# Reciprocal square roots on ACT as exp(-ln/2), and a product of queries and keys that does not wait for its masks, in a fused decoder layer

## The chip, the cores and the metric

The kernel runs on one core of a Trainium2 chip. The metric is the device time of one execution in microseconds, from the first to the last of the program's work. TensorE (PE) multiplies matrices, VectorE (DVE), ScalarE (ACT) and GpSimd (POOL) do elementwise work, and SyncE (SP) issues the transfers. Each engine has its own in-order list of instructions; engines wait for one another through semaphores.

## The reference, cut to what matters

64 sequences of 128 tokens with 512 features pass through one decoder layer: attention with 16 heads, a second mixing stage against a context (an mLSTM), a gated choice of one of eight small experts, and a layer norm after each of the three.

```python
x = _layernorm(x + attn(x, Wq, bq, Wk, bk, Wv, bv, Wo, bo))
x = _layernorm(x + mlstm(x, ctx, ctx, Wi, bi, Wf, bf, ln_scale))
x = _layernorm(x + ffn(x, ...))
# _layernorm: (x - m) / sqrt(v + 1e-5), over the 512 features
# inside mlstm, for every head:
qk = einsum('bhsd,bhtd->bhst', qh, kh) / sqrt(dh)
C = qk * D                      # D is zero above the diagonal
normalizer = maximum(abs(C.sum(-1)), exp(-max_log_D))
h = einsum('bhst,bhtd->bhsd', C / (normalizer + EPS), vh)
hn = (h - mu) * rsqrt(var + EPS)   # mean and variance over a head's 32 features
```

So a tile needs four reciprocal square roots: one per token in each of the three layer norms, and one per token and head (16 columns) in the mLSTM.

## The kernel before, in words

A tile is one sequence: 128 tokens on the partitions, 512 features in a row. Seven tiles are in flight at once. In step a the kernel works on tile a and its six elders, called b (one older) to g (six older): the projections of a, the attention of b up to its layer norm x1, the gates and the decay matrix Dx of c, the mLSTM's result of d, its layer norm x2 and the experts' products of e, their choice for f, and the last layer norm and the store for g. Nothing schedules this at run time: each engine has a hand-written `step(a)` that names the pieces in the order in which that engine does them, and the order of the five lists is what the kernel is tuned by. The first 10 steps are unrolled, the next 54 run in a loop with two steps in its body, and 6 more drain the pipeline. POOL's list is counted one step behind the others, so its `c` is the others' `d`.

In the loop a wait stands only where the code says `wait_ge`; the waits in `edge(...)` are written out in unrolled steps alone, because in the loop another wait or an engine's own order already implies them.

The pieces that the change and the prediction name:

- TensorE, at the end of a step: the projection of the keys `p_k` (L376 is its last group), `m_QK` (L478, the product of the context's queries and keys, into the four banks of `quad`), the transposes of x1 `m_x1T` (L365), the experts' first product, the next tile's transposes, the gates `m_gate` (L458, L460), and then the attention's scores `a_S` (L412 lays down a mask, L418 multiplies). In the middle of a step `m_H` (L500) makes the mLSTM's result and `x_Y` (L526) the experts' second product; L526 waits until ACT has copied the result of L500 out of its banks (`Hs`, L659).
- DVE: `norm_stats` makes mean and variance (L926, L929, and `ve` in L931), `a_x1` (L946) the normalized x1, `p_KT` (L875) a transpose, `m_C` (L969) the product of `quad` and the masked Dx, in four parts in the order 1, 3, 0, 2; `r_y` (L992) multiplies by `h_rs`.
- ACT: `m_Dx` (L652) makes Dx as 16 exponentials, `x_yo` (L690) the output row from `rs3` and `nm3`, `m_x1T` (L622) a copy.
- POOL: four powers with exponent -0.5 (L777 for 128x16, L791 for 128x1), `m_mask` (L762, the zeros above the diagonal of Dx, four parts), `r_y2` (L781), `r_r2` (L786), `x_nm` (L814, minus mean times `rs3`).

Before the first tile TensorE runs 62 small products on ones to warm up (WARM), between two steps of the set-up.

Of the kernel before, what the change touches and what calls it, by code (L numbers as in the profile page):

```python
# [27 lines left out]
P = 128  # L28
# [3 lines left out]
H = 16  # L32
# [22 lines left out]
PADS = 5  # L55
PEEL = 10
WARM = 62
# [47 lines left out]
def bass_decoder(nc, x, ctx, wq, wk, wv, wo, bqkv, bo, rope, ident, mask_l, mask_r, head_rows,  # L105
                 w_gate, b_gate, ln_scale, w_expert, debias, degen, expert_rows, out):
    with ExitStack() as stack:
# [3 lines left out]
        def sem(name):  # L111
# [23 lines left out]
        half_neg = sb("half_neg", [P, H])  # L135
# [19 lines left out]
        ve1 = sb("ve1", [P, 1])  # L155
        rs1 = sb("rs1", [P, 1])
# [28 lines left out]
        h_ve = sb("h_ve", [P, H])  # L185
        h_rs = sb("h_rs", [P, H])
# [3 lines left out]
        ve2 = sb("ve2", [P, 1])  # L190
        rs2 = sb("rs2", [P, 1])
# [26 lines left out]
        ve3 = sb("ve3", [P, 1])  # L218
        rs3 = sb("rs3", [P, 1])
# [140 lines left out]
        def _(pe):  # L360
# [223 lines left out]
        def _(act):  # L584
# [106 lines left out]

            nc.scalar.preload_act_table_set("natural_log_exp_and_others")
# [10 lines left out]
            def step(a):  # L703
# [37 lines left out]
                if b.real():  # L741
                    m_x1T(b)
# [4 lines left out]
        def _(pool):  # L747
# [53 lines left out]
            def x_score(t):  # L801
                pool.wait_ge(s.fn3_sb, upto(t))
                tt(f_s[:], f_sc[:], f_n3[:], ALU.mult).then_inc(s.fs_sb, 1)
# [3 lines left out]
                edge(pool, t, (s.fe_sb, 1))  # L807
# [9 lines left out]
            nc.gpsimd.memset(half_neg[:], -0.5).then_inc(s.pads_set, 1)  # L817
# [15 lines left out]
            def step(a):  # L833
# [13 lines left out]
                if d.real():  # L847
                    rsqrt(d, ve2, rs2, s.ve2_sb, s.rs2_sb, s.x2_sb)
# [6 lines left out]
                if c.real():  # L855
                    r_pow(c)
                if f.real():
                    rsqrt(f, ve3, rs3, s.ve3_sb, s.rs3_sb, s.yo_sb)
                    x_nm(f)
# [8 lines left out]
        def _(dve):  # L868
# [385 lines left out]
```

## Time and profile before

| what | value |
|---|---|
| runs | 1709.47, 1708.28, 1704.01 us; median 1708.28 |
| profiled execution | 1706.93 us, of which the span of the trace is 1705.2 us |
| busy over the span | PE 1520.7 us (89%), DVE 1283.2 (75%), POOL 955.2 (56%), ACT 855.4 (50%) |
| chain that ended last | POOL 31%, PE 25%, DVE 21%, issue 19% |
| stage up to 91 us | set-up and first tile, PE busy 36.19 us |
| 91 to 335 us | unrolled steps, PE busy 219.66 of 244 us |
| 335 to 1640 us | the loop, PE busy 1233.26 of 1305 us, granted clock 1.00 |
| 1640 to 1705.2 us | the drain, PE busy 31.63 of 65.2 us, granted clock 0.65 |

A busy share says how long an engine worked, not whether it set the pace: the chain follows from the last instruction back to whatever released each wait. The loop holds more than three quarters of the time and its steps are alike, so one step read closely stands for 54.

### The profile page before, as it was taken

The page shows a single profiled execution, that of the slowest core. Times are in us where ns is not written, and L with a number is a line of the kernel's source. Part 1 is how long each engine was busy: PE and PEld are TensorE (multiplying, and loading weights), DVE is VectorE, ACT ScalarE, POOL GpSimd, SP SyncE. Part 2 cuts the span into 40 slices and gives each one's busy share as a digit, 9 for nine tenths or more (in the row PEclk, how much of TensorE's full clock was granted, in tenths as well). Part 3 has the DMA queues.
Part 4 walks back from the last instruction along what each step waited for, and adds up shares of the span by engine and source line. Part 5 has one row for each costly group of instructions (what it writes and reads, how often), then busy time and mean ns, then how long its engine had stood idle before and what let it go on. Part 6 is the DMA issues. An engine that isn't in the chain of part 4 may idle for free.

```text
span 1705.2 us, 67667 instructions
## 1 busy us (share of the span) xinstructions
PE 1520.7 (89%) x27398; PEld 1196.0 (70%) x27398; DVE 1283.2 (75%) x3337; ACT 855.4 (50%) x2385; POOL 955.2 (56%) x1232
## 2 busy tenths in 40 slices
PE   0789999999999999999999999999999999999955
PEld 0667777777777777777777777777777777777743
DVE  4346777787787778777877787778778877877764
ACT  2035545545554555455545554555555455645551
POOL 1025556555655665566556655665565556556653
PEclk9899999999999999999999999999999999999985
DMA  4123333333433343333233333333343334333310
GB/s 155 38 84 106 105 105 101 108 105 99 123 103 106 99 123 98 112 99 122 96 104 109 118 99 95 120 108 105 96 123 105 105 99 123 102 108 99 105 58 31
DMA packets 195142, 174.71 MB, mean 102 GB/s; under 512 B 141887, under 2 KB 143551, under 8 KB 186890
## 3 DMA queue, kind: packets, MB, share of 16 engines
q1 hardware_dynamic: 195082, 173.87, 33.4%
q8 instruction: 42, 0.69, 0.2%
q14 instruction: 18, 0.15, 0.0%
HBM read 139.76 MB, written 34.08 MB: 102 GB/s over the span
## 4 chain that ended last, share of the span: by engine, by line
POOL 31%; PE 25%; DVE 21%; issue 19%; ACT 2%; SPq 1%; POOLq 1%; DMA 0%; DVEq 0%; ACTq 0%
POOL h_rs L777 12%; POOL Dx L762 5%; PE quad L418 5%; POOL rs L791 4%; POOL r L786 4%; DVE Dx L969 3%; PE bank L365 3%; PE bank L513 2%; PE bank L490 2%; PE bank L458 2%; PE bank L526 2%; POOL nm L814 2%; POOL c L770 2%; PE bank L373 2%; PE bank L374 2%
## 5 line engine op out<-in xcount | busy, mean ns | idle before, releaser
L757 POOL TENSOR_TENSOR ex<-ex,w_rec 128x512 f32<-128x512 f32 x64 | 67.2, 1050 | 543.7 <-DVE w_rec L910 543.7
L652 ACT ACTIVATE Dx<-Mb,a_col 128x128 f32<-128x128 f32 x1024 | 312.9, 395 | 7.6 <-DMA Mb<-m_rows 7.4
L777 POOL TENSOR_TENSOR h_rs<-h_ve,half_neg 128x16 f32<-128x16 f32 x64 | 207.1, 3236 | 8.5 <-DVE h_ve L987 1.7
L622 ACT ACTIVATE x1T<-bank 128x512 f32<-128x512 f32 x64 | 38.2, 597 | 314.4 <-PE bank L365 314.4
L762 POOL TENSOR_SCALAR_AFFINE_SELECT Dx<-Dx 128x512 f32<-128x512 f32 x256 | 159.9, 636 | 8.6 <-ACT Dx L652 8.6
L969 DVE SCALAR_TENSOR_TENSOR Dx<-quad,Dx 128x512 f32<-128x512 f32 x256 | 157.1, 668 | 7.3 <-PE quad L478 7.3
L946 DVE TENSOR_SCALAR x<-r,mv,rs 128x512 f32<-128x512 f32 x64 | 54.3, 849 | 129.6 <-POOL rs L791 129.6
L791 POOL TENSOR_TENSOR rs<-ve,half_neg 128x1 f32<-128x1 f32 x192 | 104.8, 546 | 37.7 <-DVE ve L931 37.6
L659 ACT ACTIVATE Hs<-quad 128x528 f32<-128x528 f32 x64 | 39.1, 611 | 171.3 <-PE quad L500 171.3
L478 PE MATMUL quad<-x1T,cT 32*128 32x128 f32 x2048 | 76.6, 286 | 43.3 <-issue 26.9
L373 PE MATMUL bank<-wq_high,x_high 128*128 128x512 f32 x256 | 115.1, 449 | 0.0
L373 PE MATMUL bank<-wv_high,x_high 128*128 128x512 f32 x256 | 114.3, 446 | 0.0
L478 PEld LDWEIGHTS quad<-x1T,cT 32*128 32x128 f32 x2048 | 66.0, 189 | 68.7 <-POOL Dx L762 66.3
L373 PE MATMUL bank<-wk_high,x_high 128*128 128x512 f32 x256 | 112.8, 441 | 0.0
L431 PEld LDWEIGHTS quad<-PT,VG 32*32 32x32 f32 x8192 | 74.9, 103 | 53.0 <-issue 52.3
L373 PE MATMUL bank<-wo_high,O_high 128*128 128x512 f32 x256 | 106.8, 417 | 0.0
L374 PE MATMUL bank<-wo_low,O_high 128*128 128x512 f32 x256 | 102.7, 401 | 0.0
L374 PE MATMUL bank<-wq_low,x_high 128*128 128x512 f32 x256 | 102.2, 399 | 0.0
L365 PE MATMUL bank<-id_sb,x 128*128 128x128 f32 x512 | 82.5, 284 | 21.4 <-DVE x L946 11.3
L374 PE MATMUL bank<-wk_low,x_high 128*128 128x512 f32 x256 | 101.1, 395 | 0.0
L374 PE MATMUL bank<-wv_low,x_high 128*128 128x512 f32 x256 | 100.8, 394 | 0.0
L936 DVE TENSOR_TENSOR r<-bank,xr 128x512 f32<-128x512 f32 x64 | 44.3, 692 | 73.5 <-PE bank L376 73.5
(163 smaller groups left out, 4357.4 us busy)
## 6 DMA issues: line engine op xcount, KB each, us to landing
Mb<-m_rows SPq DMA_DIRECT2D x64, 1024.0 KB, 4.6
xb<-in_x SPq DMA_DIRECT2D x256, 64.0 KB
xr<-in_x SPq DMA_DIRECT2D x64, 256.0 KB, 3.0
cb<-in_ctx SPq DMA_DIRECT2D x64, 256.0 KB, 2.6
v_rows<-v_sb SPq DMA_DIRECT2D x64, 256.0 KB, 3.3
VG<-v_rows SPq DMA_DIRECT2D x64, 256.0 KB, 3.9
out_dram<-yo SPq DMA_DIRECT2D x64, 256.0 KB, 3.1
Dx<-in_wq SPq DMA_DIRECT2D x4, 256.0 KB, 4.7
```

Source lines behind the costliest of these rows:

```text
L365: last = nc.tensor.transpose(dst[:, c * P:(c + 1) * P], src[:, c * P:(c + 1) * P], id_sb[:])
L373: mm(bank[b][:], high[:, c, :], w_high[n][:, c, :], start=first and c == 0, stop=False)
L374: mm(bank[b][:], high[:, c, :], w_low[n][:, c, :], start=False, stop=False)
L418: last = mm(quad[32 * c:32 * c + 32, w, 32 * v:32 * v + 32], QT[rows, cols], KT[rows, cols], start=False, stop=True, skip_group_check=True ...
L431: last = mm(quad[32 * w:32 * w + 32, c, 32 * v:32 * v + 32], VG[rows, w, v, :], PT[rows, w, v, :], start=True, stop=True, skip_group_check ...
L478: last = mm(quad[:, j, n * P:(n + 1) * P], cT[t.parity()][rows, n, :], x1T[t.parity()][rows, n, :], start=True, stop=True)
L652: last = go(Dx[t.parity()][:, j, n, :], Mb[t.parity()][:, h, :], ACT.Exp, bias=a_col[t.parity()][:, h:h + 1], scale=-1.0)
L762: nc.gpsimd.affine_select(Dx[t.parity()][:, j], Dx[t.parity()][:, j], compare_op=ALU.is_ge, fill=0.0, base=0, pattern=[[0, CH], [1, P]], c ...
L777: tt(h_rs[:], h_ve[:], half_neg[:], ALU.pow).then_inc(s.hrs_sb, 1)
L786: tt(r2[:], r2[:], x1[t.parity()][:], ALU.add).then_inc(s.r2_sb, 1)
L791: tt(rs[:], ve[:], half_neg[:, 0:1], ALU.pow).then_inc(rs_sem, 1)
L969: stt(out=Dx[t.parity()][:, j], in0=quad[:, j, :].rearrange("p (c n) -> p c n", n=P), scalar=float(D) ** -0.5, in1=Dx[t.parity()][:, j], o ...
```

## The change

The four powers leave POOL. In their place ACT computes ln(ve) into a new small tile and then exp(-0.5 ln), as two activations joined by a semaphore. `n_2` stands on ACT ahead of `m_Hs`, `n_h` behind the first quarter of Dx, `n_3` behind the copy of x2's transposes, `n_1` at the end of the step ahead of the copy of x1's transposes. `m_QK` no longer waits for the masks. On POOL the fourth mask now directly follows the third, mask 2 of the next tile stands ahead of `r_y2`, and `x_nm` stands behind it. Two waits that the old order implied are written out: x1 waits for the addition r2 of two tiles before, and POOL's score for the previous exponential. There are 68 warming products in place of 62, and one memset fewer.

```diff
-PADS = 5
+PADS = 4
-WARM = 62
+WARM = 68
             def m_QK(t):
-                for j in range(3):
-                    pe.wait_ge(s.Dm_sb[j], upto(t))
                 edge(pe, t, (s.x1T_sb, 0), (s.cT_sb, 0), (s.sub_sb, -1), (s.Ohigh_sb, -1), (s.Olow_sb, -1))
...
+            def rsqrt(t, ve, ln, rs, ve_sem, ln_sem, rs_sem, used):
+                act.wait_ge(ve_sem, upto(t))
+                go(ln[:], ve[:], ACT.Ln).then_inc(ln_sem, 1)
+                act.wait_ge(ln_sem, upto(t))
+                edge(act, t, (used, 1))
+                go(rs[:], ln[:], ACT.Exp, scale=-0.5).then_inc(rs_sem, 1)
+            def n_1(t):
+                rsqrt(t, ve1, ln1, rs1, s.ve1_sb, s.ln1_sb, s.rs1_sb, s.x1_sb)
...
-            def r_pow(t):
-                pool.wait_ge(s.hve_sb, upto(t))
-                edge(pool, t, (s.y1_sb, 1))
-                tt(h_rs[:], h_ve[:], half_neg[:], ALU.pow).then_inc(s.hrs_sb, 1)
-            def rsqrt(t, ve, rs, ve_sem, rs_sem, used):
-                pool.wait_ge(ve_sem, upto(t))
-                edge(pool, t, (used, 1))
-                tt(rs[:], ve[:], half_neg[:, 0:1], ALU.pow).then_inc(rs_sem, 1)
             def x_score(t):
                 pool.wait_ge(s.fn3_sb, upto(t))
+                pool.wait_ge(s.fe_sb, upto(t, 1))
...
-            nc.gpsimd.memset(half_neg[:], -0.5).then_inc(s.pads_set, 1)
             def a_x1(t):
                 dve.wait_ge(s.rs1_sb, upto(t))
-                edge(dve, t, (s.r2_sb, 2), (s.x1T_ps, 2))
+                dve.wait_ge(s.r2_sb, upto(t, 2))
+                edge(dve, t, (s.x1T_ps, 2))
```

On ACT, in the loop, around the copy Hs of the mLSTM's result (HT, ex and cT are other copies and the attention's exponential; ve is the variance of x2's norm). Before:

```order
L617 ACTIVATE HT<-bank 128x512 [waits HT_ps]
L601 ACTIVATE ex<-ex 128x512 [waits sub_sb]
L659 ACTIVATE Hs<-quad 128x528 [waits H_ps]
L612 ACTIVATE cT<-bank 128x512 [waits cT_ps]
L664 ACTIVATE h_abs<-Hs 128x16 [waits Hs_sb]
```

and after, the same stretch:

```order
L618 ACTIVATE HT<-bank 128x512 [waits HT_ps]
L602 ACTIVATE ex<-ex 128x512 [waits sub_sb]
L695 ACTIVATE ln<-ve 128x1 [waits ve2_sb]
L698 ACTIVATE rs<-ln 128x1 [waits ln2_sb]
L660 ACTIVATE Hs<-quad 128x528 [waits H_ps]
L613 ACTIVATE cT<-bank 128x512 [waits cT_ps]
L665 ACTIVATE h_abs<-Hs 128x16 [waits Hs_sb]
```

Two activations, the first with a wait for ve2, stand ahead of Hs. On ACT at the end of a step, from the copy of x2's transposes on. Before:

```order
L674 ACTIVATE x2T<-bank 128x512 [waits x2T_ps]
L595 REGISTER_ALU [waits v_ps]
L596 ACTIVATE v_sb<-bank 128x512 [waits v_out]
L652 ACTIVATE Dx<-Mb,a_col 128x128 x4
L689 REGISTER_ALU [waits nm3_sb]
L690 ACTIVATE yo<-y_0,nm,rs 128x512 [waits y_out]
L622 ACTIVATE x1T<-bank 128x512 [waits x1T_ps]
```

and after:

```order
L675 ACTIVATE x2T<-bank 128x512 [waits x2T_ps]
L695 ACTIVATE ln<-ve 128x1 [waits ve3_sb]
L698 ACTIVATE rs<-ln 128x1 [waits ln3_sb]
L596 REGISTER_ALU [waits v_ps]
L597 ACTIVATE v_sb<-bank 128x512 [waits v_out]
L653 ACTIVATE Dx<-Mb,a_col 128x128 x4
L690 REGISTER_ALU [waits nm3_sb]
L691 ACTIVATE yo<-y_0,nm,rs 128x512 [waits y_out]
L695 ACTIVATE ln<-ve 128x1 [waits ve1_sb]
L698 ACTIVATE rs<-ln 128x1 [waits ln1_sb]
L623 ACTIVATE x1T<-bank 128x512 [waits x1T_ps]
```

The pair for the last norm stands ahead of the copy of v, the pair for x1 behind yo. On POOL, in the loop, from the context's product c to the masks (h_rs and rs are the powers, r the mLSTM's result on its way to x2). Before:

```order
L770 TENSOR_TENSOR c_1<-cb,a_col 128x16x31 [waits HT_ps,c_in1,acol_sb]
L777 TENSOR_TENSOR h_rs<-h_ve,half_neg 128x16 [waits hve_sb]
L789 REGISTER_ALU
L791 TENSOR_TENSOR rs<-ve,half_neg 128x1 [waits ve3_sb]
L814 TENSOR_SCALAR nm<-mv,rs 128x1 [waits rs3_sb,pads_set]
L781 TENSOR_TENSOR r<-r,lns_sb 128x512 [waits y1_sb]
L762 AFFINE_SELECT Dx<-Dx 128x512 [waits Dx_sb2,pads_set]
L786 TENSOR_TENSOR r<-r,x_0 128x512 [waits x1_sb,y2_sb]
L762 AFFINE_SELECT Dx<-Dx 128x512 [waits Dx_sb0,pads_set]
L762 AFFINE_SELECT Dx<-Dx 128x512 [waits Dx_sb1,pads_set]
L791 TENSOR_TENSOR rs<-ve,half_neg 128x1 [waits ve1_sb]
```

and after:

```order
L798 TENSOR_TENSOR c_1<-cb,a_col 128x16x31 [waits HT_ps,c_in1,acol_sb]
L790 AFFINE_SELECT Dx<-Dx 128x512 [waits Dx_sb2,pads_set]
L804 TENSOR_TENSOR r<-r,lns_sb 128x512 [waits y1_sb]
L832 TENSOR_SCALAR nm<-mv,rs 128x1 [waits rs3_sb,pads_set]
L809 TENSOR_TENSOR r<-r,x_0 128x512 [waits x1_sb,y2_sb]
L790 AFFINE_SELECT Dx<-Dx 128x512 [waits Dx_sb0,pads_set]
L790 AFFINE_SELECT Dx<-Dx 128x512 [waits Dx_sb1,pads_set]
L790 AFFINE_SELECT Dx<-Dx 128x512 [waits Dx_sb3,pads_set]
```

The powers are gone, mask 2 has moved ahead of the multiplication by lns_sb and nm behind it. TensorE's list differs only in the waits of L478 and in the count of warming products.

## Rows read from the trace of the kernel before

**Rows 1.** One step: stretch, length, busy PE, PEld, DVE, ACT, POOL, clock, DMA, GB/s

```profile
1004.69:1029.20 24.51, 23.14 (x427) 18.38 (x428) 19.54 (x51) 13.19 (x37) 14.84 (x20) 1.00 0.36 110
```

**Rows 2.** Waits in 52 loop steps: total us, times, longest us

```profile
PE quad L478 <- issue: 24.5, 41, 0.6
...
PE quad L412 <- DVE Dx L969: 9.3, 26, 0.4
PE bank L365 <- DVE x L946: 8.7, 51, 0.2
...
PE quad L478 <- POOL Dx L762: 6.9, 11, 0.6
```

**Rows 3.** Timeline of TensorE, end of a step: start, us, line, operation, idle before

```profile
1002.98 1.08 PE L376 MATMUL bank<-wk_high,x_low 128*128 128x512 f32 x4
1004.69 1.17 PE L478 MATMUL quad<-x1T,cT 32*128 32x128 f32 x32 [0.63 <-POOL Dx L762]
...
1008.90 0.27 PE L460 MATMUL bank<-cT,wg_ctx 128*48 128x128 f32 x1
1009.53 0.24 PE L412 MATMUL quad<-pair_r,pair_l 32*128 32x128 bf16 x4 [0.36 <-DVE Dx L969]
```

**Rows 4.** Timeline of POOL in the same step

```profile
995.72 3.24 POOL L777 TENSOR_TENSOR h_rs<-h_ve,half_neg 128x16 f32<-128x16 f32 x1
...
999.66 0.64 POOL L814 TENSOR_SCALAR nm<-mv,rs 128x1 f32<-128x1 f32 x1 [0.18 <-POOL rs L791]
1000.26 1.29 POOL L781 TENSOR_TENSOR r<-r,lns_sb 128x512 f32<-128x512 f32 x1
...
1002.12 1.29 POOL L786 TENSOR_TENSOR r<-r,x 128x512 f32<-128x512 f32 x1
1003.36 1.23 POOL L762 TENSOR_SCALAR_AFFINE_SELECT Dx<-Dx 128x512 f32<-128x512 f32 x2
```

**Rows 5.** Timeline of TensorE, first step of the loop

```profile
341.72 1.08 PE L376 MATMUL bank<-wk_high,x_low 128*128 128x512 f32 x4
342.73 1.17 PE L478 MATMUL quad<-x1T,cT 32*128 32x128 f32 x32
```

**Rows 6.** Timeline of DVE in the step of rows 3

```profile
991.27 0.15 DVE L931 TENSOR_SCALAR ve<-mv 128x1 f32<-128x1 f32 x1
...
999.48 0.68 DVE L992 TENSOR_TENSOR r<-Hs,h_rs 128x512 f32<-128x512 f32 x1
...
1002.83 0.15 DVE L931 TENSOR_SCALAR ve<-mv 128x1 f32<-128x1 f32 x1
1005.13 0.84 DVE L946 TENSOR_SCALAR x<-r,mv,rs 128x512 f32<-128x512 f32 x1 [2.15 <-POOL rs L791]
1005.90 1.07 DVE L875 STREAM_TRANSPOSE KT<-bank 128x512 f32<-128x512 f32 x1
1006.83 2.44 DVE L969 SCALAR_TENSOR_TENSOR Dx<-quad,Dx 128x512 f32<-128x512 f32 x4
```

**Rows 7.** Timeline of ACT in the same step

```profile
986.30 0.31 ACT L633 ACTIVATE g_exp<-g_abs 16x128 f32<-16x128 f32 x1
...
986.85 0.29 ACT L637 ACTIVATE g_ln<-g_exp 16x128 f32<-16x128 f32 x1
...
991.63 0.61 ACT L659 ACTIVATE Hs<-quad 128x528 f32<-128x528 f32 x1 [2.73 <-PE quad L500]
...
994.22 0.18 ACT L643 ACTIVATE eFM<-bank 128x16 f32<-128x16 f32 x1
...
1000.92 0.82 ACT L690 ACTIVATE yo<-y,nm,rs 128x512 f32<-128x512 f32 x1
```

**Rows 8.** Timeline of TensorE, the experts' product of the same step

```profile
992.39 1.10 PE L526 MATMUL bank<-degen_sb,LT 72*128 72x512 f32 x2 [0.17 <-ACT Hs L659]
```

**Rows 9.** Timeline of ACT, start of the kernel

```profile
0.81 1.28 ACT L692 ACT_TABLE_LOAD   x1 [0.81 <-PEq L1245]
```

**Rows 10.** Timeline of TensorE, warming products

```profile
42.34 6.47 PE L532 MATMUL bank<-ones_bf 128*128 128x128 bf16 x62 [42.34 <-DVE wx_prod L1123]
```

More of the change, by code:

```diff
@@ L134, in bass_decoder @@
         xrow_sb = sb("xrow_sb", [P, 3, NX])
-        half_neg = sb("half_neg", [P, H])
         xb = [sb(f"xb{i}", [P, E]) for i in range(2)]
@@ L155, in bass_decoder @@
         ve1 = sb("ve1", [P, 1])
+        ln1 = sb("ln1", [P, 1])
         rs1 = sb("rs1", [P, 1])
@@ L185, in bass_decoder @@
         h_ve = sb("h_ve", [P, H])
+        h_ln = sb("h_ln", [P, H])
         h_rs = sb("h_rs", [P, H])
@@ L190, in bass_decoder @@
         ve2 = sb("ve2", [P, 1])
+        ln2 = sb("ln2", [P, 1])
         rs2 = sb("rs2", [P, 1])
@@ L218, in bass_decoder @@
         ve3 = sb("ve3", [P, 1])
+        ln3 = sb("ln3", [P, 1])
         rs3 = sb("rs3", [P, 1])
@@ L229, in bass_decoder @@
             S_ps max_sb sub_sb ex_sb sum_sb rec_sb exn_sb PT_sb
-            O_ps Ohigh_sb Olow_sb proj_ps r1_sb st1_sb mv1_sb ve1_sb rs1_sb x1_sb
+            O_ps Ohigh_sb Olow_sb proj_ps r1_sb st1_sb mv1_sb ve1_sb ln1_sb rs1_sb x1_sb
             x1T_ps x1T_sb cT_ps cT_sb c1_sb gate_ps gs_sb gsum_sb gabs_sb gexp_sb gln_sb
             Fs_sb a_sb M_sb FM_sb aT_ps acol_sb QK_ps HT_ps HT_sb H_ps Hs_sb sq_sb
-            habs_sb hn1_sb hn2_sb hnn_sb hvar_sb hve_sb hrs_sb y1_sb y2_sb r2_sb
-            st2_sb mv2_sb ve2_sb rs2_sb x2_sb rs2sq_sb
+            habs_sb hn1_sb hn2_sb hnn_sb hvar_sb hve_sb hln_sb hrs_sb y1_sb y2_sb r2_sb
+            st2_sb mv2_sb ve2_sb ln2_sb rs2_sb x2_sb rs2sq_sb
             x2T_ps x2T_sb F_ps fz_sb fz2_sb fn1_sb fn2_sb fn3_sb fs_sb fu_sb fv_sb fe_sb fe1_sb
             gate_sb gmax_sb gkey_sb gkmax_sb oh_sb L_sb LT_ps LT_sb Y_ps y3_sb st3_sb mv3_sb
-            ve3_sb rs3_sb nm3_sb yo_sb""".split()
+            ve3_sb ln3_sb rs3_sb nm3_sb yo_sb""".split()
         four = "Dx_sb Dm_sb C_sb".split()
@@ L690, in x_yo, with n_h, n_2, n_3 @@
                 go(yo[:], y3[t.parity()][:], ACT.Identity, bias=nm3[:], scale=rs3[:]).then_inc(s.yo_sb, 1)
+            def rsqrt(t, ve, ln, rs, ve_sem, ln_sem, rs_sem, used):
[6 more added lines that the diff above has]
+                rsqrt(t, ve1, ln1, rs1, s.ve1_sb, s.ln1_sb, s.rs1_sb, s.x1_sb)
+            def n_h(t):
+                rsqrt(t, h_ve, h_ln, h_rs, s.hve_sb, s.hln_sb, s.hrs_sb, s.y1_sb)
+            def n_2(t):
+                rsqrt(t, ve2, ln2, rs2, s.ve2_sb, s.ln2_sb, s.rs2_sb, s.x2_sb)
+            def n_3(t):
+                rsqrt(t, ve3, ln3, rs3, s.ve3_sb, s.ln3_sb, s.rs3_sb, s.yo_sb)
             nc.scalar.preload_act_table_set("natural_log_exp_and_others")
@@ L715, in step @@
                     a_exp(b)
+                if e.real():
+                    n_2(e)
                 if d.real():
@@ L730, in step @@
                     m_Dx(c, 2)
+                if d.real():
+                    n_h(d)
+                if c.real():
                     m_Dx(c, 0)
@@ L734, in step @@
                     x_x2T(e)
+                if g.real():
+                    n_3(g)
                 if a.real():
@@ L741, in step @@
                 if b.real():
+                    n_1(b)
                     m_x1T(b)
@@ L806, in x_score @@
                 pool.wait_ge(s.fu_sb, upto(t))
-                edge(pool, t, (s.fe_sb, 1))
                 tt(f_v[:], f_u[:], xrow_sb[:, 1, :], ALU.mult).then_inc(s.fv_sb, 1)
@@ L839, in step @@
                     m_mask(c, 1)
-                if b.real():
-                    rsqrt(b, ve1, rs1, s.ve1_sb, s.rs1_sb, s.x1_sb)
-                if c.real():
                     m_mask(c, 3)
@@ L846, in step @@
                     a_scale(a)
-                if d.real():
-                    rsqrt(d, ve2, rs2, s.ve2_sb, s.rs2_sb, s.x2_sb)
                 if e.real():
@@ L854, in step @@
                     m_c1(b)
[L855 to L859, printed above, removed]
+                if b.real():
+                    m_mask(b, 2)
                 if c.real():
                     r_y2(c)
-                if b.real():
-                    m_mask(b, 2)
+                if f.real():
+                    x_nm(f)
             steps(pool, step)
```

## Prediction

> **What bounds the kernel now.** I read the busy time of one step first, then the table of waits over the loop, then the timelines of one step engine by engine. One pass of the loop body for one tile lasts 24.51 us, and TensorE is busy in 23.14 of them at granted clock 1.00, so at its full level of 2.4 GHz [rows 1]. The kernel is therefore nearly TensorE bound, and only TensorE's holes can be won: 24.51 - 23.14 = 1.37 us a step. The waits say whose they are [rows 2]. Over 52 steps TensorE stands idle before the product of queries and keys (L478) for 24.5 + 6.9 = 31.4 us, 0.60 a step; before the transposes of x1 8.7 us, 0.17 a step; before the attention scores (L412), held by DVE's product with Dx, 9.3 us, 0.18 a step. In the timeline of one step the last product ends at 1002.98 + 1.08 = 1004.06, L478 starts at 1004.69 [rows 3]; POOL's masks 0 and 1 end at 1003.36 + 1.23 = 1004.59 [rows 4]. So L478 waits for the masks, though "issue" is named in 41 of 52 steps. Of the masks' lateness POOL's power of 3.24 us is one link, but the multiplication by lns_sb (L781) that follows waits for DVE as well: DVE's r ends at 999.48 + 0.68 = 1000.16, L781 starts at 1000.26 [rows 4, 6].
>
> **The change part by part.** All times are on the axis of that one step.
>
> Product without masks: how L478 starts when the masks are already there is shown at the loop's first step: the product before it ends at 341.72 + 1.08 = 342.80 and L478 starts at 342.73, 0.07 before that end [rows 5]. So the term is 0.60 + 0.07 = 0.67 us a step. Bounds: 0.53, were it to start 0.07 behind instead, and 0.70 from the step shown (1004.69 - 1003.99). What is late next is x1.
>
> x1 and the scores: x1 starts at 1005.13 after 2.15 us of waiting for POOL's rs, which lies behind the masks [rows 6]. Its variance is ready at 1002.83 + 0.15 = 1002.98. The new pair, Ln and Exp of 128x1, stands on ACT after yo. The nearest row is an Exp of 128x16 at 0.18 us; the dearest are Exp and Ln of 16x128 at 0.31 and 0.29 [rows 7]. With three handovers of at most 0.10 (DVE's r to POOL's L781, above) the pair takes 0.45 to 0.90 us; I take 0.5, nearer to the 128x16 row. ACT must be free: yo now waits for nm, which stands behind L781: 1000.26 + 1.29 + 0.64 = 1002.19, and yo takes 0.82, to 1003.05 with a handover. rs would then be there at 1003.5 to 1003.6. x1 has a new wait too, r2 of two tiles before: L781, nm and the addition L786 one after the other, 1000.26 + 1.29 + 0.64 + 1.29 = 1003.48, with a handover 1003.58 [rows 4]. Both paths end at 1003.6, so x1 moves 1.5 us forward. Behind it on DVE are the transpose KT (0.77 later) and Dx (0.93 after that) [rows 6]: Dx could start at 1005.30. L478 would end at 1003.99 + 1.17 = 1005.16, so x1's transposes find their input: 0.17 saved, and 0.07 for the same running together of two products. The masks 0 and 1 end at 1003.48 + 1.23 = 1004.71, before DVE wants them. The scores: before, Dx ends at 1006.83 + 2.44 = 1009.27 and L412 starts at 1009.53, 0.26 later, while the gate's products end at 1008.90 + 0.27 = 1009.17 [rows 3, 6]. After, Dx ends at 1007.74 and would let L412 go at 1008.00; TensorE gets there at 1005.16 + (1009.17 - 1005.86 - 0.17) - 0.07 = 1008.23, less 0.07. So TensorE is last again and the 0.18 go, with 0.07: 0.25. DVE's spare time there is only 0.16 us, which is the thin place of this forecast.
>
> What it costs: n_2's pair stands on ACT ahead of Hs, and Hs holds TensorE: the experts' product L526 waits 0.17 us for it [rows 8]. ve2 is ready at 991.27 + 0.15 = 991.42, Hs starts at 991.63 [rows 6, 7]. With 0.04 to 0.10 to hand over, two activations of 0.18 and a step between them, Hs starts at 991.77 if it overlaps with the Exp and at 991.95 if not: 0.14 to 0.32 later; I take 0.20. With the dear rows it would be 0.5; below nothing it can't be, since no work is taken off ACT. The other two pairs lie beside slack: h_rs is wanted by DVE's r at 999.48, and POOL took its variance up at 995.72, so ACT has 3.8 us for it; rs3 is wanted after L781, at 1000.26 + 1.29 = 1001.55. On POOL the power of 3.24 us and three of one column go, on ACT 8 x 0.18 = 1.4 us of busy time come; POOL's saving is worth nothing by itself, since L781 still waits for DVE's r at the same place.
>
> What a table would cost is weighed here too. The trace has one table load, 1.28 us, at the start of ACT [rows 9], and Exp L633 and Ln L637 lie 0.55 us apart in start with another activation between [rows 7]: no load fits. The Trainium skill, "ScalarE: Activation LUTs", section "Table sets: the hidden batching unit", says that one set is active at a time and that natural_log_exp_and_others has both Exp and Ln. The trace agrees; by that page ("What ACT_TABLE_LOAD costs") a change of set would be 2.66 us, an estimated 21 us for eight a step, had they lain in two sets.
>
> Start: six more warming products. 62 of them take 6.47 us [rows 10], so six take 0.63 us, and the copy that follows is on DVE's way to the weights' low parts, so I count them: +0.6, bounds 0 and 0.63.
>
> The sum: per step -0.67 - 0.24 - 0.25 + 0.20 = -0.96 us. The loop has 54 steps: -51.8. The eight unrolled steps with this product and the drain get, as an estimate from the same terms, -3 (bounds 0, since code is issued less evenly there, and -13, all terms in full). With the start: -54. The profiled execution took 1706.93 us (span 1705.2, the 1.7 around it unchanged): 1653. Its time lies between the lowest run (1704.0) and the median (1708.3); against the median the sum gives 1654. I say 1653.
>
> **Rivals.** First, the wait moves to x1 on DVE. For it: yo, r2 and rs all end within 0.1 us of each other, and only 0.16 us is spare. Against it: each of these was added with its full duration. If x1 comes half a microsecond later (1004.1), L412 starts 0.34 later: -0.62 a step, -33 in the loop, -2 outside, 1672. At 1.0 us later the step saves 0.12 and the time is 1698.
>
> Second, the masks hold the end as before. DVE's Dx needs them whatever TensorE does, and they still follow L781 and L786. They would have to end 0.75 us (1005.30 - 1004.71 + 0.16) later than worked out to undo anything; then the scores wait where the product waited, and at 0.96 more all is as before: 1707. Little speaks for it, since POOL has one power fewer in that stretch.
>
> Third, slower: ACT holds TensorE. ACT works in order, and Hs, the context's copy, O_high and all of Dx now stand behind a wait for ve2. At present ve2 is 0.21 us ahead of Hs. The gains other than this are 0.67 + 0.24 + 0.25 = 1.16 us; the kernel is slower once Hs starts more than 1.16 us later, so once ve2 comes 0.84 (1.16 - 0.32) us later against TensorE. At 1.5 us later Hs slips 1.82 us: -1.16 + 1.82 = +0.66 a step, +36, 1743. Against it: DVE's rows from the scores to ve2 follow one another without the change touching any of them, and r2, which the statistics need, is written at 1003.41 now, 12 us before ve2's next turn.
>
> Fourth, slower by tables: eight loads of 1.28 us [rows 9] are 10.2 us of ACT a step, two of them ahead of Hs: -1.16 + 0.20 + 2.56 = +1.6 a step, 1793. Only the row speaks of the price, nothing for the case.
>
> **How the numbers follow.** The forecast gets 0.70, the wait moved to x1 0.20, the masks 0.04, ACT holding TensorE 0.05, tables 0.01. The forecast alone: -1.16 + 0.14 a step with -13 outside gives 1639; the dear pair (0.5 for Hs) gives -0.66 a step and, with nothing outside, 1671. A cheaper start of L412 in full (0.36 in the step shown) is inside the first. The range reaches into the first rival: 1638 to 1682, with about 1 in 10 above it and somewhat less below. A change of 0.3% is 5 us, about what a measurement of this kernel can tell from none. Faster: 0.70 + 0.18 of the first rival = 0.88; same: 0.02 + 0.03 = 0.05; slower: 0.05 + 0.01 + 0.01 = 0.07.
>
> **What would show it.** In the changed kernel's timeline L478 should start within 0.1 us of the product's end, with 0.6 us gone; the step should be 23.5 to 23.6 us. x1 should start about 1.5 us earlier against the product's end, and its wait should name ACT's rs or POOL's r2. L412 should follow the gate's products without a wait for Dx. Hs should start 0.1 to 0.3 us later against ve2, and L526's wait grow from 0.17 to about 0.37. POOL should be busy for less than 14.84 - 3.24 = 11.6 us a step, ACT for about 13.19 + 1.4 = 14.6. The forecast is wrong if TensorE still shows a wait of 0.3 us or more before L412 or x1's transposes (first rival), if L412 waits for masks (second), or if L526's wait is over 1 us (third).

## The result and the profile after

The changed kernel takes 1634.1 us (median of 1634.38, 1636.49, 1633.84 and 1633.58), the kernel before 1708.9 beside it: a ratio of 0.956 [0.952, 0.960]. The forecast was 1653 with a range from 1638 to 1682. The direction and the place were right, the size was not: the gain is 75 us, where 54 were forecast.

The page of the changed kernel, busy times of the engines and the chain of waits:

```profile
PE 1503.2 (92%) x27277; PEld 1192.3 (73%) x27404; DVE 1284.0 (79%) x3337; ACT 947.2 (58%) x2897; POOL 629.5 (39%) x975
...
PE 72%; DVE 18%; issue 5%; ACT 4%; SPq 1%; DMA 0%; POOL 0%; DVEq 0%; POOLq 0%
```

POOL, 31% of the chain before, is off it; TensorE has gone from 25% to 72%. One step of the loop, in the columns of [rows 1], with which it compares:

```profile
984.18:1007.50 23.32, 22.95 (x428) 18.32 (x429) 19.63 (x52) 14.62 (x45) 9.84 (x16) 1.00 0.37 112
```

A step is 1.2 us shorter (24.51 before). POOL lost 5.0 us of busy time and ACT took 1.4. Of the waits of TensorE over the loop [rows 2] one kind is left that counts:

```profile
PE bank L527 <- ACT Hs L660: 14.5, 51, 0.3
```

The end of a step on TensorE (L479 was L478, L368 was L365, L415 was L412, L463 was L460), to set beside [rows 3]:

```profile
983.15 1.10 PE L379 MATMUL bank<-wk_high,x_low 128*128 128x512 f32 x4
984.18 1.17 PE L479 MATMUL quad<-x1T,cT 32*128 32x128 f32 x32
985.28 0.66 PE L368 MATMUL bank<-id_sb,x 128*128 128x128 f32 x4
...
988.15 0.27 PE L463 MATMUL bank<-cT,wg_ctx 128*48 128x128 f32 x1
988.36 0.23 PE L415 MATMUL quad<-pair_r,pair_l 32*128 32x128 bf16 x4
```

L479 starts 0.07 us before the key product's end (983.15 + 1.10 = 984.25), the transposes 0.07 before L479's, the scores 0.06 before the gate's (988.42). All three holes are closed. DVE and POOL in the same stretch, beside [rows 6] and [rows 4]:

```profile
982.99 0.15 DVE L940 TENSOR_SCALAR ve<-mv 128x1 f32<-128x1 f32 x1
983.65 0.98 DVE L956 TENSOR_SCALAR x<-r,mv,rs 128x512 f32<-128x512 f32 x1 [0.51 <-ACT rs L698]
984.55 1.06 DVE L884 STREAM_TRANSPOSE KT<-bank 128x512 f32<-128x512 f32 x1
985.48 1.85 DVE L979 SCALAR_TENSOR_TENSOR Dx<-quad,Dx 128x512 f32<-128x512 f32 x3
```

```profile
980.38 1.30 POOL L804 TENSOR_TENSOR r<-r,lns_sb 128x512 f32<-128x512 f32 x1 [2.81 <-DVE r L1002]
981.65 0.27 POOL L832 TENSOR_SCALAR nm<-mv,rs 128x1 f32<-128x1 f32 x1
981.88 1.30 POOL L809 TENSOR_TENSOR r<-r,x 128x512 f32<-128x512 f32 x1
983.12 2.00 POOL L790 TENSOR_SCALAR_AFFINE_SELECT Dx<-Dx 128x512 f32<-128x512 f32 x3
```

x1 waits 0.51 us for its scale, where it waited 2.15 [rows 6]. The second of the three masks of the last row ends at about 984.45 (two thirds of 2.00), 0.2 us behind the key product: it is still late for L479, which only no longer waits for it. ACT, the pair ahead of Hs and the pair for x1:

```profile
971.51 0.20 ACT L695 ACTIVATE ln<-ve 128x1 f32<-128x1 f32 x1 [2.55 <-DVE ve L940]
971.74 0.20 ACT L698 ACTIVATE rs<-ln 128x1 f32<-128x1 f32 x1
971.85 0.59 ACT L660 ACTIVATE Hs<-quad 128x528 f32<-128x528 f32 x1
...
983.18 0.20 ACT L695 ACTIVATE ln<-ve 128x1 f32<-128x1 f32 x1 [0.32 <-DVE ve L940]
983.41 0.20 ACT L698 ACTIVATE rs<-ln 128x1 f32<-128x1 f32 x1
```

Each activation of 128x1 takes 0.20 us, the second starts 0.23 behind the first, and an activation that doesn't depend on the second (Hs) starts 0.11 behind it.

Where the 72.5 us between the two spans came from is read at one instruction of every step, DVE's addition that begins x1's norm. Before, at tiles 0, 9, 10, 62 and 63:

```profile
86.97 0.69 DVE L936 TENSOR_TENSOR r<-bank,xr 128x512 f32<-128x512 f32 x1 [5.82 <-PE bank L376]
...
312.66 0.69 DVE L936 TENSOR_TENSOR r<-bank,xr 128x512 f32<-128x512 f32 x1 [0.99 <-PE bank L376]
...
339.83 0.69 DVE L936 TENSOR_TENSOR r<-bank,xr 128x512 f32<-128x512 f32 x1 [1.67 <-PE bank L376]
...
1614.16 0.69 DVE L936 TENSOR_TENSOR r<-bank,xr 128x512 f32<-128x512 f32 x1 [0.95 <-PE bank L376]
...
1639.61 0.69 DVE L936 TENSOR_TENSOR r<-bank,xr 128x512 f32<-128x512 f32 x1 [2.09 <-PE bank L376]
```

and after:

```profile
86.71 0.69 DVE L945 TENSOR_TENSOR r<-bank,xr 128x512 f32<-128x512 f32 x1 [4.44 <-PE bank L379]
...
302.48 0.69 DVE L945 TENSOR_TENSOR r<-bank,xr 128x512 f32<-128x512 f32 x1 [1.05 <-PE bank L379]
...
328.41 0.69 DVE L945 TENSOR_TENSOR r<-bank,xr 128x512 f32<-128x512 f32 x1 [1.48 <-PE bank L379]
...
1540.85 0.69 DVE L945 TENSOR_TENSOR r<-bank,xr 128x512 f32<-128x512 f32 x1 [0.97 <-PE bank L379]
...
1567.32 0.69 DVE L945 TENSOR_TENSOR r<-bank,xr 128x512 f32<-128x512 f32 x1 [1.60 <-PE bank L379]
```

The start gives 0.3 us; the nine unrolled steps 225.69 - 215.77 = 9.9; the 53 steps from tile 9 to tile 62, which lie in the loop, 1301.50 - 1238.37 = 63.1, 1.19 each; the step from tile 62 to tile 63 loses 1.0 and the drain gains 0.2. (The loop is longer than the stretch from 335 to 1640 us that I had called by its name: TensorE's branch at the end of a pass stands at 345.2 for the first time and at 1620.3 for the last, so the loop begins at about 295. The step of [rows 5] is the second of the loop's first pass.)

### The profile page after: what moved, and what is told of

It is laid out like the page before. It is cut to its first block, busy times and chain, and to the rows that moved or that the text cites. A ratio compares the mean times of both kernels' runs of the same rounds, so it can differ in the third digit from the quotient of the medians.

```text
span 1632.7 us, 67814 instructions
## 1 busy us (share of the span) xinstructions
PE 1503.2 (92%) x27277; PEld 1192.3 (73%) x27404; DVE 1284.0 (79%) x3337; ACT 947.2 (58%) x2897; POOL 629.5 (39%) x975
## 4 chain that ended last, share of the span: by engine, by line
PE 72%; DVE 18%; issue 5%; ACT 4%; SPq 1%; DMA 0%; POOL 0%; DVEq 0%; POOLq 0%
PE bank L376 13%; PE bank L377 12%; PE bank L379 11%; PE bank L368 6%; PE quad L421 5%; PE quad L434 5%; PE bank L527 5%; PE quad L479 4%; PE bank L461 4%; PE bank L514 4%; DVE w_sum L914 2%; DVE neg_max L905 2%; DVE ex L910 2%; DVE st L935 2%; ACT Hs L660 2%
## 5 line engine op out<-in xcount | busy, mean ns | idle before, releaser
L653 ACT ACTIVATE Dx<-Mb,a_col 128x128 f32<-128x128 f32 x1024 | 317.6, 388 | 4.1 <-DMA Mb<-m_rows 4.1
L790 POOL TENSOR_SCALAR_AFFINE_SELECT Dx<-Dx 128x512 f32<-128x512 f32 x256 | 167.2, 677 | 89.4 <-ACT Dx L653 89.4
L695 ACT ACTIVATE ln<-ve 128x1 f32<-128x1 f32 x192 | 38.1, 199 | 198.2 <-DVE ve L940 198.2
L804 POOL TENSOR_TENSOR r<-r,lns_sb 128x512 f32<-128x512 f32 x64 | 82.6, 1291 | 173.5 <-DVE r L1002 109.2
L527 PE MATMUL bank<-degen_sb,LT 72*128 72x512 f32 x128 | 76.0, 677 | 20.5 <-ACT Hs L660 15.2
L368 PE MATMUL bank<-id_sb,x 128*128 128x128 f32 x512 | 82.4, 284 | 9.2 <-DVE x2sq L1018 7.0
L421 PE MATMUL quad<-KT,QT 32*32 32x32 f32 x8192 | 83.4, 200 | 5.8 <-issue 5.8
L434 PE MATMUL quad<-PT,VG 32*32 32x32 f32 x8192 | 82.8, 201 | 6.2 <-issue 5.9
L935 DVE BATCH_NORM_STATS2 st<-r 128x6 f32<-128x512 f32 x128 | 85.3, 666 | 3.9 <-POOL r L809 1.6
```

What stands on the lines that cost most here:

```text
L368: last = nc.tensor.transpose(dst[:, c * P:(c + 1) * P], src[:, c * P:(c + 1) * P], id_sb[:])
L421: last = mm(quad[32 * c:32 * c + 32, w, 32 * v:32 * v + 32], QT[rows, cols], KT[rows, cols], start=False, stop=True, skip_group_check=True ...
L434: last = mm(quad[32 * w:32 * w + 32, c, 32 * v:32 * v + 32], VG[rows, w, v, :], PT[rows, w, v, :], start=True, stop=True, skip_group_check ...
L527: mm(bank[6][:], LT[:], degen_sb[:], start=True, stop=True).then_inc(s.Y_ps, 1)
L653: last = go(Dx[t.parity()][:, j, n, :], Mb[t.parity()][:, h, :], ACT.Exp, bias=a_col[t.parity()][:, h:h + 1], scale=-1.0)
L790: nc.gpsimd.affine_select(Dx[t.parity()][:, j], Dx[t.parity()][:, j], compare_op=ALU.is_ge, fill=0.0, base=0, pattern=[[0, CH], [1, P]], c ...
```

## The experiments

My theory was: x1's chain (its power, x1, the transpose KT, Dx, the scores) and the wait for the masks held TensorE in two places that lie one behind the other, so that taking out the first wait gains nothing without the second edit; what is left is the pair ahead of Hs; and POOL's lighter load is worth nothing by itself. The rivals: the parts add up; POOL's lighter load carries part of the gain.

**The mask wait alone.** The kernel before, without the waits; the two waits that the old order implied (for r2 at x1, and for the previous exponential at POOL's score) are written out as in the changed kernel:

```diff
 def m_QK(t):
-    for j in range(3):
-        pe.wait_ge(s.Dm_sb[j], upto(t))
...
```

> The kernel before, with all four powers left on POOL, and only the waits of the product of queries and keys for the masks taken out. Theory (the two edits work only together): the product starts 0.67 us earlier in each step, but the transposes of x1 behind it still wait for x1, whose power stands behind the masks on POOL; the engine's idle time moves from the one place to the other, and the end of the step stays: 1708 us, within 4 us. Rival (the parts add up): 54 x 0.67 = 36 us are gained by this edit alone: 1672 us.

Measured: 1712.3 us, ratio 1.0017 [1.0001, 1.0034]. Nothing is gained. Its waits of TensorE, tiles 10 to 62:

```profile
PE bank L365 <- DVE x L945: 43.7, 51, 0.9
PE quad L412 <- DVE Dx L968: 9.5, 26, 0.4
```

The hole before the product is gone, and the one before x1's transposes has grown from 8.7 [rows 2] to 43.7 us: 35 us, what the mask wait had cost. The step stays at 24.5 us.

**x1's power alone on ACT.** The kernel of the first experiment, thus without the mask wait, with x1's power off POOL and its Ln and Exp on ACT at the changed kernel's place; the three other powers stay on POOL:

```diff
+def n_1(t):
+    act.wait_ge(s.ve1_sb, upto(t))
+    go(ln1[:], ve1[:], ACT.Ln).then_inc(s.ln1_sb, 1)
+    act.wait_ge(s.ln1_sb, upto(t))
+    edge(act, t, (s.x1_sb, 1))
+    go(rs1[:], ln1[:], ACT.Exp, scale=-0.5).then_inc(s.rs1_sb, 1)
...
```

> The kernel before without the mask waits, and with only the power of x1's norm on ACT as Ln and Exp; the powers of the other three norms stay on POOL. Theory: what gains is x1's power leaving its place behind the masks, together with the earlier product: key product, x1's transposes and the scores give 0.68 + 0.24 + 0.3 in each step, and the experts' product no longer waits behind a second pair on ACT (0.11 us back): 1628 us (1624 to 1636). Rival (POOL's freeing as a whole is needed: its 3.24 us for the 16 columns delay the masks, and with them the scores): half of the gain or less is there, 1670 us or more.

Measured: 1627.35 us, 0.9516 [0.9491, 0.9542]. A step of its loop, in the columns of [rows 1]:

```profile
980.35:1003.53 23.18, 22.94 (x428) 18.32 (x427) 19.71 (x52) 13.62 (x39) 14.36 (x20) 1.00 0.36 115
```

One power out of four, with the mask wait gone, gives the whole gain and 7 us more, with POOL nearly as busy as before the change (14.36 us a step, 14.84 before). The 7 us are what the pair ahead of Hs costs, as the run that moves it shows below.

**The power of 16 columns back on POOL**, in the changed kernel; its pair on ACT goes:

```diff
-def n_h(t):
-    rsqrt(t, h_ve, h_ln, h_rs, s.hve_sb, s.hln_sb, s.hrs_sb, s.y1_sb)
...
+def r_pow(t):
+    pool.wait_ge(s.hve_sb, upto(t))
+    edge(pool, t, (s.y1_sb, 1))
+    tt(h_rs[:], h_ve[:], half_neg[:], ALU.pow).then_inc(s.hrs_sb, 1)
...
```

> The changed kernel with the power of the 16 columns (3.24 us on POOL in the kernel before) put back on POOL, the other three norms staying on ACT. Theory: POOL is idle for 60% of the span in the changed kernel, and its 3.24 us are not on the path: 1634 us within 3. Rival (the gain over the forecast comes from POOL having less to do, through the masks or through what POOL and DVE take from each other): 3.2 us of POOL in each step come back on the masks and the scores, at 0.3 us a step or more: 1650 us or more.

Measured: 1634.2 us, 0.957 [0.9557, 0.9583]. The step stays at 23.32 us with POOL busy for 13.04 of it in place of 9.84:

```profile
984.18:1007.50 23.32, 22.95 (x435) 18.32 (x428) 19.86 (x52) 14.31 (x43) 13.04 (x17) 1.00 0.38 111
```

So the rival that POOL's load counts falls for the changed kernel, where the product doesn't wait for the masks: 3.2 us of it a step change nothing. With that wait kept it is otherwise, as a run below shows.

**The price of a pair ahead of Hs, from both sides.** First a second, unused pair there, then the only pair moved behind Hs:

```diff
 def n_2(t):
+    act.wait_ge(s.ve2_sb, upto(t))
+    act.wait_ge(s.rs2b_sb, upto(t, 1))
+    go(ln2b[:], ve2[:], ACT.Ln).then_inc(s.ln2b_sb, 1)
+    act.wait_ge(s.ln2b_sb, upto(t))
+    go(rs2b[:], ln2b[:], ACT.Exp, scale=-0.5).then_inc(s.rs2b_sb, 1)
+    act.wait_ge(s.rs2b_sb, upto(t))
     rsqrt(t, ve2, ln2, rs2, s.ve2_sb, s.ln2_sb, s.rs2_sb, s.x2_sb)
```

> The changed kernel with a second pair of Ln and Exp of the same 128 values (its result unused) ahead of x2's pair, thus ahead of the scaling of the hidden sums (Hs). Theory: Hs ends the wait of the experts' product, so that what ACT does ahead of it stands on the path: a pair took 0.20 + 0.20, its own start-to-start 0.23 to 0.34 us: 53 x 0.23 to 0.40 = 12 to 21 us, 1650 us (1646 to 1655). Rival (TensorE has slack there, or other work covers it): 1634 us.

Measured: 1662.2 us, 0.9723 [0.9696, 0.975]: 28 us more than the changed kernel, above the 12 to 21 expected. Its ACT, and TensorE's wait for Hs (total us, times, longest):

```profile
986.16 0.20 ACT L711 ACTIVATE ln2b<-ve 128x1 f32<-128x1 f32 x1 [2.54 <-DVE ve L948]
986.39 0.20 ACT L713 ACTIVATE rs2b<-ln2b 128x1 f32<-128x1 f32 x1
986.63 0.20 ACT L697 ACTIVATE ln<-ve 128x1 f32<-128x1 f32 x1
986.86 0.20 ACT L700 ACTIVATE rs<-ln 128x1 f32<-128x1 f32 x1
986.97 0.59 ACT L662 ACTIVATE Hs<-quad 128x528 f32<-128x528 f32 x1
```

```profile
PE bank L529 <- ACT Hs L662: 39.2, 49, 0.8
```

The extra pair costs 0.47 us from its start to that of the next (986.63 - 986.16), because the edit makes the next pair wait for the extra one's result (the wait for `rs2b_sb`). The experts' product waits 39.2 / 49 = 0.80 us in place of 0.28, and 54 x 0.52 = 28 us: all of the loss is there.

```diff
 (in ACT's step)
-n_2(e)
 m_Hs(d)
+n_2(e)
```

> The changed kernel with x2's Ln and Exp moved on ACT from just ahead of the scaling of the hidden sums (Hs) to just behind it. Theory: Hs started 0.11 us after the Exp of the pair, and the sums that it reads were done at 971.68, 0.17 us before it started at 971.85; so it starts 0.11 to 0.17 us earlier in each step and the experts' product with it, while x2 comes some 0.6 us later, which has room: 54 x 0.11 = 6 us less, 1628 us (1625 to 1631). Rival (x2 and its transposes become the wait): 1634 us or more, up to 1634 + 54 x 0.5 = 1661 us.

Measured: 1627.9 us, 0.9533 [0.952, 0.9546], as the theory has it; the wait for Hs goes back to 0.17 us a step:

```profile
PE bank L527 <- ACT Hs L660: 8.3, 50, 0.2
```

**The wait for Hs where Hs stands in the way.** The changed kernel with TensorE's wait at the output product `a_O`, one place later:

```diff
 def a_O(t):
...
+    pe.wait_ge(s.Hs_sb, upto(t, 2))
...
 def x_Y(t):
...
-    pe.wait_ge(s.Hs_sb, upto(t, -3))
```

> The changed kernel with TensorE's wait for the scaled hidden sums (Hs) moved from the experts' product to the output product that really reads them, which stands behind it. Theory: the 0.27 to 0.29 us that the experts' product waits in each step are covered by its own work, and by the time of the output product Hs is long done: 53 x 0.27 = 14 us less, 1620 us (1617 to 1625). Rival (the output product or what is behind it then waits as long for another engine): 1634 us.

Measured: 1617.2 us, 0.947 [0.9457, 0.9483]: the fastest kernel here, 17 us below the changed one. The reason in one row, a step of its loop:

```profile
912.34:935.32 22.98, 22.98 (x427) 18.29 (x427) 19.79 (x51) 14.66 (x45) 9.73 (x15) 1.00 0.40 114
```

TensorE is busy for all of it. With only x1's power on ACT as well (and 62 warming products, as in the kernel before):

> Two of the better versions together: of the four powers only x1's is on ACT, and TensorE's wait for the scaled hidden sums stands at the output product. Theory: TensorE no longer waits in the loop in the version with the moved wait alone, so that nothing is left for ACT's shorter list to give: 1617 us (1614 to 1620). Rival (the three powers left on POOL delay its masks and sums enough to hold TensorE again): 1625 us or more.

Measured: 1620.8 us, 0.9477 [0.9462, 0.9492], just above the 1614 to 1620 expected; the two intervals overlap, so that nothing is gained. From tile 9 to tile 62 both kernels take the same, 1224.5 and 1224.2 us: the loop has no more waits to give.

**The powers on ACT, with the mask wait kept.** The changed kernel with the three waits of `m_QK` put back:

> The changed kernel, with the waits for the masks put back ahead of the product of queries and keys. Theory: by the changed kernel's rows the third mask of the three that are waited for ends at about 984.45 (the last three begin at 983.12 and take 2.00 together), the product starts at 984.18, so that each step is longer by 0.25 to 0.35 us and nothing behind it makes up for that: 54 x 0.3 = 16 us, 1650 us (1646 to 1656). Rival (the parts add up, and each gain belongs to one edit): the whole 0.68 of a step comes back, 1634 + 37 = 1671 us. Second rival (the masks aren't on the path any more, since POOL has less to do): 1634 us.

Measured: 1750.5 us (1729 to 1753), a ratio of 1.0193 [1.0123, 1.0262]. No theory had it. Its instruction queue and a stretch of TensorE's timeline:

```profile
q8 instruction: 159, 2.61, 0.7%
```

```profile
478.07 0.27 PE L523 MATMUL bank<-id_sb,L 128*72 128x128 f32 x1
482.37 1.11 PE L368 MATMUL bank<-id_sb,xb 128*128 128x128 f32 x4 [4.03 <-issue]
483.41 0.45 PE L461 MATMUL bank<-x1T,wg_sb 128*48 128x128 f32 x1
```

```profile
478.34:482.37 4.03, 0.00 (x0) 0.01 (x1) 1.19 (x4) 0.00 (x0) 0.00 (x0) 0.76 0.03 4
482.37:487.00 4.63, 4.63 (x152) 3.73 (x152) 0.98 (x2) 1.77 (x5) 0.00 (x0) 0.50 0.01 4
```

At the top of the loop, between the last product of one pass and the first of the next, TensorE stands still for 4 us with no engine to wait for, the other engines run dry, and the granted clock falls to 0.50, 1.2 GHz: a gate's product takes 0.45 in place of 0.31. The queue has 159 packets of instructions, where the kernels before and after have 42 each. So three more runs: this kernel with one wait in place of three, this kernel with 62 warming products in place of 68, and the kernel before with 68.

```diff
-    for j in range(3):
-        pe.wait_ge(s.Dm_sb[j], upto(t))
+    pe.wait_ge(s.Dm_sb[1], upto(t))
```

> The changed kernel with one wait of the product of queries and keys for mask 1, the last of the three to be made, in place of the three waits that cost 116 us in the run with all three. In that run TensorE stood still for 4.0 us at the top of the loop, with no engine to wait for, in about half of the loop's passes, ran at half its clock behind it, and 159 packets of instructions were loaded in place of 42; its other passes took 46.80 us for two steps against 46.63. Theory (the wait itself is cheap, the loss is the loading of TensorE's code, which two instructions fewer a step avoid): 54 x 0.085 = 5 us more than the changed kernel, 1639 us (1634 to 1645), 42 packets. Rival (the wait for the mask causes the standstill): 1700 us or more, with over 100 packets.

```diff
-WARM = 68
+WARM = 62
```

> The changed kernel with all three mask waits and 62 warming products, which gives TensorE the very list of instructions of the kernel before. Theory A (the place of the loop in TensorE's code decides; six products are twelve instructions ahead of it, and the kernel before shows no loading in its loop): 42 packets of instructions, 1639 us (1634 to 1646). Theory B (the length of the loop decides, together with the shorter step): over 100 packets, 1730 to 1755 us.

> The kernel before with 68 warming products in place of 62, nothing else. TensorE's list is then that of the changed kernel with the three mask waits put back. Theory A (the place of the loop in TensorE's code decides whether it is loaded again): over 100 packets of instructions and, at some 4 us for each of the standstills, 1740 us or more. Theory B (length and the shorter step decide): 42 packets, 1709 us within 3.

Measured: 1648.8 us, 0.965 [0.9631, 0.9669], with one wait; 1651.6, 0.9668 [0.965, 0.9686], with three waits and 62; 1753.2, 1.0262 [1.0209, 1.0315], for the kernel before with 68. The queues of the three, in this order:

```profile
q8 instruction: 42, 0.69, 0.2%
```

```profile
q8 instruction: 42, 0.69, 0.2%
```

```profile
q8 instruction: 96, 1.57, 0.4%
```

and TensorE in the last:

```profile
494.61 0.27 PE L520 MATMUL bank<-id_sb,L 128*72 128x128 f32 x1
499.60 0.68 PE L365 MATMUL bank<-id_sb,xb 128*128 128x128 f32 x2 [4.71 <-issue]
```

Six small products ahead of the loop, which are cheap where they stand, cost the kernel before 44 us through its loop. The packets came out as the theory of the place has it (96, a little under the 100 that I had put down for the last run), but the first two times lie above the ranges that I had given for it, 1634 to 1645 and 1634 to 1646. Loading again shows only where both the 68 products and the three waits a step are there (two kernels); with 62 products and three waits (two, the kernel before among them), with 68 and one wait or none (six, the changed kernel among them), and with 62 and none (four), there are 42 packets. The waits count for the place too, because the unrolled steps have them as well: ahead of the loop TensorE's list has 355 instructions beside its products and weight loads with three waits a step, 347 with one, and 339 or fewer with none, and six products with their weight loads are twelve. Against the kernel before, the loop thus begins 12 instructions later in the two kernels that load again, and from 20 earlier to 4 later in the twelve that don't. So the place of the loop is enough to tell all 14 apart. Whether its length counts beside that isn't shown: a pass is two instructions shorter without the three waits, and no run changes that alone. This would fit a loop whose end must not pass some place in the code, but the traces don't say whose code a packet holds, so it stays a reading. What is shown: with the three waits kept, six more products ahead of the loop bring the packets and the standstills, whether the powers are on POOL or on ACT.

Where nothing is loaded again, the mask wait can be priced: 1648.8 and 1651.6 against 1634.1 are 15 and 17 us. The theory of the first of these runs had 16, but not from the right places: it put 0.25 to 0.35 us on each step of the loop, and a step is longer by 0.16 us with one wait (23.48 on the mean) and by 0.21 with three (23.53), some 9 and 11 us; the rest lies outside the loop. That the totals agree is partly luck. (The 5 us that I put down afterwards, from the undisturbed passes of the disturbed kernel, were too few.)

And the rest of the change, with the three waits kept, makes 1651.6 of 1708.9: 57 of the 75 us. So the second edit does gain without the first. A part of that is POOL's after all: in this kernel, whose TensorE list is that of the kernel before, the product starts 0.15 us behind the end of the one ahead of it, in place of 0.63 [rows 3]:

```profile
990.70 1.10 PE L379 MATMUL bank<-wk_high,x_low 128*128 128x512 f32 x4
991.95 1.17 PE L481 MATMUL quad<-x1T,cT 32*128 32x128 f32 x32 [0.15 <-issue]
```

On the mean of the loop's steps the stretch from the attention's output product to this one is 0.46 us shorter than before, some 25 us in 54 steps, because the masks come earlier against it. Whether the powers that left POOL or its new order of work brings that, no run separates; nor was x1's power alone on ACT tried with the mask wait kept. Once the product no longer waits for the masks, these 25 us come with that edit anyway, and POOL's load is worth nothing.

**The warming products** of the changed kernel, 62 again:

> The changed kernel with 62 instead of 68 products that warm TensorE before the first tile. Theory: the 68 took 6.02 us from 43.04 and the 62 of the kernel before 6.47 from 42.34, so that six more cost nothing that can be seen: 1634 us within 1. Rival (the prediction's term): 0.6 us less, 1633.4 us; second rival (fewer products, and the clock rises later): up to some us more.

Measured: 1638.3 us, 0.9585 [0.9571, 0.9599], 4 us above the 1634 within 1 that I had expected. The interval overlaps with that of the run with the power back on POOL, made beside it and equal to the changed kernel (0.957 [0.9557, 0.9583]), so that the 4 us are at the edge of what can be told. Its steps in the loop are 23.32 us as in the changed kernel, and its nine unrolled steps 219.3 in place of 215.8. Among the eight kernels that have x1's power on ACT and no mask wait, the nine unrolled steps take 214.2 to 215.8 us in the five with 68 products and 217.6 to 221.0 in the three with 62, each in one profiled execution; in the kernel before it is the other way round (225.7 with 62, 227.3 with 68). So the rival with some us more for fewer products isn't ruled out, and what moves the unrolled part stays open. In the changed kernel the 68 take less than the 62 before [rows 10]:

```profile
43.04 6.02 PE L533 MATMUL bank<-ones_bf 128*128 128x128 bf16 x68 [43.04 <-DVE wx_prod L1133]
```

But the scatter is as large as the term: 62 products take 5.1 to 6.5 us in the six kernels that have them, 68 take 5.6 to 6.5 in the eight others.

## Why the prediction was too small

- **The product without masks** (0.67 a step): right. It starts 0.07 before the product ahead of it ends, as the step of [rows 5] showed.
- **x1's transposes** (0.24): right, 1.10 us from L479 to L368 in place of 1.34.
- **x1's chain**: rs was forecast for 1003.5 to 1003.6 on the axis of before, 0.52 to 0.62 behind ve; x1 started 983.65 - 983.14 = 0.51 behind it. Of the paths that I had ending together only the pair's set this: ACT stood idle for 0.32 ahead of Ln, and r2 ended 0.04 behind ve (981.88 + 1.30 = 983.18) in place of the 0.50 that I had worked out. No row names x1 or Dx ahead of the scores, so neither the rival with the wait at x1 nor the one with the masks came true; nor did the two slower ones, as L527 waits 0.29 us and no table is loaded behind the start.
- **POOL and ACT** (under 11.6 us and about 14.6 busy a step): 9.84 and 14.62, and with the mask wait gone POOL's saving is worth nothing by itself, as the run with 13.04 showed.
- **The scores** (0.25): undersized, and this is the term at which the range failed. In the step shown L478 and L412 start 1009.53 - 1004.69 = 4.84 us apart [rows 3], and 4.84 in the other step of a pass as well: in both DVE's Dx sets the time. After, it is 988.36 - 984.18 = 4.18 in both: 0.66 less, where the sum had 0.24 + 0.25 = 0.49. My own timeline had it right, 1008.23 - 0.07 - 1003.99 = 4.17; the sum took the mean of a table of waits instead, 9.3 us over 52 steps [rows 2]. That table has only every second step under this name. In the others L412 waited too, about 0.14 us, which the view gives in part to "issue" and in part not at all, and the rest of the time up to Dx was hidden in a hole at the loop's top (below). L415 now overlaps with the gate by 0.06, so the wait itself gives (0.36 + 0.14) / 2 + 0.06 = 0.31.
- **Hs** (+0.20 taken): oversized. It grew from 0.17 [rows 8] to 0.29, so +0.12: the overlapping case, 0.14, which I had as a bound. The pair moved behind Hs gave 6 us back, 0.12 a step; an unused pair ahead of it cost more, 0.52, since there each of the two pairs waits for the one before.
- **The loop's top**: not in the sum. Before, the load of the next tile's transposes waited at the top of every second step, where the pass begins (columns: total us, times, longest):

```profile
PEld bank L365 <- issue: 6.0, 24, 0.3
```

(From 330 to 1500 us.) The changed kernel has no such row there, and from x1's transposes to the gate's end each of its steps takes 3.14 us; before, every second took 3.35. The kernel without the mask wait alone, whose x1 transposes still wait, keeps the row (5.8 us in 24); the two kernels with the mask wait, the powers on ACT and 42 packets, whose x1 transposes don't wait, have no such row. So the hole goes when x1's transposes stop waiting, perhaps since TensorE's sequencer then reaches the branch before the work ahead of it is done; the link is in the traces, the reason is argued and not shown. It is 0.10 a step.

Together the step moved by -0.67 - 0.24 - 0.31 - 0.10 + 0.12 = -1.20 in place of -0.96. Over the loop that is 63.1 us in place of 51.8, 11 us more. **Outside the loop** the change gave 9.9 + 0.3 - 1.0 + 0.2 = 9.4 us, where I had 3 less 0.6, 7 us more; with these 18 us the forecast would have been 1635. This is the second step that failed: I gave the unrolled steps and the drain 3 us, near the lower bound, for fear of uneven code issue, while the upper bound of 13 said "all terms in full". The nine unrolled steps gained 1.1 us each, close to the loop's 1.2, but that they follow the loop isn't shown: they gain 6.4 us with 62 warming products, 4.7 to 11.5 in the eight kernels named above, and 3.7 in the kernel without the mask wait, whose loop gains nothing. The start was to cost 0.6 and gave 0.3, which is within the scatter of the warming products.

The range failed at its lower end, 1638: that had all terms in full outside the loop, so the 3 us are not what put the time outside it. It kept the scores at 0.25 and no hole at the loop's top; these 0.17 us a step, 9 us over the loop, are what it lacked.

The trace after has one table load, at the start of ACT, and Ln and Exp follow each other 0.22 to 0.34 us apart in all 256 pairs. The Trainium skill ("ScalarE: Activation LUTs", section "Table sets: the hidden batching unit") says that `natural_log_exp_and_others` has both, and the trace agrees.

## What to carry to other kernels

When two waits on the bounding engine lie one behind the other, price them as one chain: taking out the first alone gave nothing here, the rest of the change without it 57 us, and both 75. When the two steps of a pass are held by the same thing, take the time from one fixed point to the next out of the timeline, for both; a mean over a table of waits misses what the table leaves out or gives another name. The unrolled copies of a step are a term with a spread of its own: here they gained from 4.7 to 11.5 us. Once an engine is busy for nearly all of a step, look where each of its last waits is written: one moved by one product was worth 17 us. And when a loop's code is shifted, look at the packets of the instruction queue.

## What the hardware did that I had not expected

- Six more products ahead of a loop brought 96 packets of instructions in place of 42, standstills of some 5 us at the top of 6 of the 27 passes, +44 us; with the powers on ACT 159 packets, some 4 us in 13 passes, and 99 us more than the same kernel with 62 (1750.5 against 1651.6). Behind the standstill shown of the kernel with 159 packets TensorE runs at granted clock 0.50 for the 4.6 us of the stretch above; behind that of the kernel before with 68 the mean is 0.55 over 5.0 us.
- POOL's nm of 128x1 takes 0.27 us in the changed kernel and took 0.64 [rows 4] with operands of the same shape. It goes with the place in the list: in the five kernels where nm stands right behind POOL's own power, whose result it reads, the median is 0.54 to 0.62 us, in the nine where it stands behind the multiplication by lns_sb 0.26 to 0.27. What in that place makes it longer wasn't tried.
